# Placing every large SBUF buffer at a multiple of 64 bytes in a transformer block

## The reference

```python
mod = silu(c) @ ada_w.T + ada_b          # six vectors: shift, scale, gate for attention and for the MLP
h = rmsnorm(x) * g1 * (1 + scale_msa) + shift_msa
q, k, v = split(h @ qkv_w.T + qkv_b)     # q and k normalised per head, q scaled by 36 ** -0.5
o = softmax(q @ k.T) @ v
x = x + tanh(gate_msa) * (o @ proj_w.T + proj_b)
h2 = rmsnorm(x) * g2 * (1 + scale_mlp) + shift_mlp
x = x + tanh(gate_mlp) * (gelu(h2 @ fc1_w.T + fc1_b) @ fc2_w.T + fc2_b)
```

## Time and profile before

| | us |
|---|---|
| median of 3 runs | 3046.84 (3044.69 to 3047.96) |
| the profiled execution | 3046.41 |
| its span, first to last instruction | 3044.6 |
| TensorE matmul busy | 2963.3 (97%) |
| ScalarE busy | 1575.1 (52%) |
| VectorE busy | 1205.4 (40%) |
| GpSimd busy | 205.5 (7%) |
| mean granted clock of TensorE | 0.984 |

### The profile page before, as it was taken

The page is one execution under the profiler, slowest core; times in us unless marked ns, Lnnn a source line. Parts: engine busy times, 40 slices in busy tenths (PEclk is TensorE's granted clock), DMA queues, the critical chain, the costliest instruction groups (busy, mean ns, idle before and its releaser), DMA issues.

```text
span 3044.6 us, 36177 instructions
## 1 busy us (share of the span) xinstructions
PE 2963.3 (97%) x12968; PEld 1904.1 (63%) x12968; DVE 1205.4 (40%) x1540; ACT 1575.1 (52%) x1918; POOL 205.5 (7%) x126
## 2 busy tenths in 40 slices
PE   7999996999999999999999999999999999999998
PEld 7898993444444444444444444478888888888886
DVE  6878772333323323323323323434243342424332
ACT  3423323666666666666666666634343443434342
POOL 3232303520000000000000000000000000000000
PEclk7999997999999999999999999999999999999999
DMA  5454545232221222221222222121222222222121
GB/s 209 142 191 160 171 132 190 73 99 69 71 79 55 71 79 69 71 78 55 71 79 69 71 79 92 61 98 61 97 87 70 82 75 74 92 96 87 39 70 44
DMA packets 215540, 278.24 MB, mean 91 GB/s; under 512 B 15984, under 2 KB 125040, under 8 KB 214384
## 3 DMA queue, kind: packets, MB, share of 16 engines
q1 hardware_dynamic: 210160, 266.11, 27.4%
q10 hardware_dynamic: 5248, 10.49, 1.0%
HBM read 191.86 MB, written 84.67 MB: 91 GB/s over the span
## 4 chain that ended last, share of the span: by engine, by line
PE 80%; DVE 2%; DMA 1%; ACT 1%; SPq 0%; issue 0%; POOL 0%; DVEq 0%; POOLq 0%
PE ps L1255 23%; PE ps L1244 17%; PE ps L1305 15%; PE ps L1292 14%; PE ps L1254 7%; PE ps L1270 4%; ACT gated L1030 1%; DVE x L1162 0%; DMA vp<-v_scratch 0%; DVE rlb L1107 0%; DMA w_raw<-w 0%; DMA l_scratch<-osb 0%; DVE rlb L1101 0%; DVE w_lo L1156 0%; DVE x L1166 0%; DMA rlb<-l_scratch 0%
## 5 line engine op out<-in xcount | busy, mean ns | idle before, releaser
L983 ACT ACTIVATE prob<-ps 128x1024 f32<-128x1024 f32 x1084 | 979.4, 979 | 508.7 <-PE ps L1244 508.7
L1254 PE MATMUL ps<-prob,vp 128*64 128x512 f32 x2048 | 949.8, 601 | 1.4 <-DMA vp<-v_scratch 0.7
L1255 PE MATMUL ps<-prob,vp 128*37 128x512 f32 x2048 | 942.7, 598 | 0.0
L1244 PE MATMUL ps<-qT,kT 110*128 110x512 f32 x2048 | 564.4, 412 | 20.7 <-DMA qT<-m_scratch 19.4
L1244 PEld LDWEIGHTS ps<-qT,kT 110*128 110x128 f32 x2048 | 360.9, 189 | 346.4 <-ACT prob L983 193.5
L1255 PEld LDWEIGHTS ps<-prob,vp 128*37 128x37 f32 x2048 | 207.3, 114 | 389.2 <-issue 389.2
L1018 ACT ACTIVATE act<-ps,f1b_t 128x512 f32<-128x512 f32 x144 | 99.3, 689 | 518.8 <-PE ps L1292 518.8
L1095 DVE COPY osb<-ps 101x512 f32<-101x512 f32 x64 | 44.3, 692 | 753.4 <-PE ps L1255 750.2
L1254 PEld LDWEIGHTS ps<-prob,vp 128*64 128x64 f32 x2048 | 254.2, 136 | 118.4 <-issue 111.6
L1101 DVE RECIPROCAL rlb<-rlb 101x256 f32<-101x256 f32 x128 | 215.3, 1724 | 253.7 <-DMA rlb<-l_scratch 253.6
L1209 DVE TENSOR_TENSOR a_lo<-act,a_hi 128x512 fp32r<-128x512 f32 x144 | 99.6, 691 | 544.0 <-ACT a_hi L1020 544.0
(11 more groups left out here) (148 smaller groups left out, 2927.6 us busy)
## 6 DMA issues: line engine op xcount, KB each, us to landing
w_raw<-w SPq DMA_DIRECT2D x144, 320.0 KB, 2.8
qk_hi_scratch<-aw SPq DMA_DIRECT2D x32, 576.0 KB, 3.1
qk_lo_scratch<-aw SPq DMA_DIRECT2D x32, 576.0 KB, 4.4
kT<-qk_hi_scratch SPq DMA_DIRECT2D x128, 144.0 KB
qT<-qk_hi_scratch SPq DMA_DIRECT2D x128, 144.0 KB
v_scratch<-stv SPq DMA_DIRECT2D x32, 512.0 KB, 2.6
vp<-v_scratch SPq DMA_DIRECT2D x16, 1024.0 KB, 6.2
xb<-xT SPq DMA_DIRECT2D x8, 1280.0 KB, 10.0
```

Source lines behind the costliest of these rows:

```text
L983: act.activation(prob[:, slot, h0 * BLK:h1 * BLK], src, ACT.Exp).then_inc(exp_done, 1)
L1244: mm = pe.matmul(out, kT[r][:, h, kt * P:(kt + 1) * P], qT[:, c % 2, h], start=True, stop=True)
L1254: pe.matmul(O[0:64], vp[r][:, kt, 0:64], prob[:, j, 0:BLK], start=kt == 0, stop=kt == NT - 1)
L1255: pe.matmul(O[64:VW], vp[r][:, kt, 64:VW], prob[:, j, BLK:2 * BLK], start=kt == 0, stop=kt == NT - 1).then_inc(pv_mm, 1)
```

## The change

```diff
         def sb(stack, name, shape, dt=F32):
-            return stack.enter_context(nc.sbuf_tensor(name, shape, dt))
+            return stack.enter_context(nc.sbuf_tensor(name, shape, dt, align_bytes=64 if np.prod(shape[1:]) >= P else 32))
...
-    top = nc.sbuf_top
-    low_end = (nc.sbuf_base + 31) // 32 * 32
+    top = nc.sbuf_top // 64 * 64
+    low_end = (nc.sbuf_base + 63) // 64 * 64
...
     def following(name, shape, dt=F32):
         offset = here[0]
-        here[0] = offset + (4 * int(np.prod(shape[1:])) + 31) // 32 * 32
+        here[0] = offset + (4 * int(np.prod(shape[1:])) + 63) // 64 * 64
         return nc.alloc_sbuf_tensor_at(name, shape, dt, offset=offset)
...
     mo = following("mo", [P, 2 * NT])
+    SQ = here[0]
     mqx = following("mqx", [HD, P])
     mrow = following("mrow", [2 * NT, P])
+    here[0] = SQ
     sq0 = following("sq0", [P, 2, BLK], F32R)
```

## The result

| | before | changed |
|---|---|---|
| median of 10 runs, us | 3046.35 | 3037.99 |
| lowest to highest | 3043.76 to 3049.34 | 3034.03 to 3039.56 |
| the profiled execution, its span | 3046.41, 3044.6 | 3036.84, 3035.0 |
| ratio to before | | 0.9972, 95% interval 0.9963 to 0.9981 |

The change makes the kernel faster by 8.4 us (0.28%); 18 us had been forecast. The time lies in the wide range of 3020 to 3049 that was given, and outside the 3024 to 3034 of the forecast itself.

The account below looks back on a forecast made before the run. TensorE's matmul starts were taken to bound the MLP stage: fc2 13.4, fc1 3.8 and proj 0.8 us gave 18.0, all else 0, so 3046.84 - 18 = 3028.8 us. Range 3020 to 3049, the forecast's own 3024 to 3034.

Parts of the forecast that it names:

- the mismatch between weights and moving operand: MLP stage: fc2's weights start at 32, its moving operand at 0; this makes its step 233.3 ns, not 226.7.
- its bank order: fc2 changes its PSUM bank every three matmuls; the other possible cause of its slow step, which the prediction argued against.
- 13.4: MLP stage, fc2: 144 blocks falling from a mean of 3.267 to 3.174 us, 13.4 us saved.
- fc1's 3.8 us: MLP stage, fc1: 100 blocks of 3.21 and 36 of 3.18 us all falling to 3.174, 3.8 us saved.
- proj's 0.8: MLP stage, proj: 30 blocks falling from 3.20 to 3.174 us, 0.8 us saved.
- no new wait: MLP stage: about 1 us of cover is left between fc1 and fc2, so TensorE waits for nothing new.
- the 18.0 us: MLP stage: the savings of fc2, fc1 and proj together; every other stage was taken at 0 us.
- Rival 1: The change moves nothing TensorE feels: bank order or a coarser grid keeps fc2 slow; 3046.8 us within 2, chance 0.30.
- The argument from the qkv stage: For rival 1: half the qkv moving operands are 64 bytes off over 128, and 16.7 ns is the mean of 13.3 and 20.0.
- Rival 3: Mismatch gets worse: in a grid of 128 fc2 goes from 32 to 64 off, its price doubling; +13.5 us, 3060 us, chance 0.10.

Follow-up runs that it names:

- `qkv_only`: The kernel before with only the `sb` buffers at multiples of 64 and `main_phase` as before; ratio 0.9999.
- `w1_off_32`: The kernel before with 32 unused bytes before `w1_hi`, which also moves the buffers behind it, `a_hi` and `a_lo` among them; ratio 0.9998.
- `a_at_w2`: The kernel before with 224 unused bytes after `act32`, so only `a_hi` and `a_lo` move, nothing aligned at 64; 3038.52 against 3047.52 us, ratio 0.9970.
- the probe: The changed kernel plus runs of 24 matmuls behind the last fc2, at varied operand starts and widths (two such kernels); 226.7 ns a matmul at distance 0.
- `all_224`: The kernel before with attention and MLP buffers counted from below moved up 224 bytes, `sq0` overlapped as in the change; 3033.4 us, ratio 0.9952.
- `all_192`: The changed kernel with all buffers counted up from below moved up by 192 bytes; 3035.6 us, ratio 0.9956 to before.
- `all_128`: The changed kernel with the top at a multiple of 128 and the buffers from below moved up by 128 bytes; 3032.9 us, ratio 0.9951 to before.
- `top_128`: The changed kernel with the top of SBUF rounded to 128 bytes instead of 64; 3043.5 us, ratio 0.9985 to before.

## Why the prediction was right in sign and wrong in size

**What bounds the kernel, and that other edits cost nothing: right.** Attention, ScalarE, VectorE and the DMAs are unchanged, and `qkv_only` is at 1.00. The whole difference is fc2 and the blocks around it.

**That the mismatch between weights and moving operand makes fc2 slow, not its bank order: right, and now shown.** `w1_off_32` gives fc1 the slow step, `a_at_w2` takes it from fc2 with nothing more aligned, and two banks in turn cost nothing in the probe. The earlier trace rows had pointed to it.

**The step that failed: "With all operands of fc2 and proj at multiples of 64 I let every block of 14 run at 226.7 ns".** I took the difference in a grid of 64 bytes, so that a multiple of 64 on both sides would be a match. The grid is 256. After the change fc2's distance is 192, not 0, and its step went from 233.3 to 229.0 ns, 4.3 of the 6.7. Its blocks are 3.21 us, which is 144 x (3.267 - 3.213) = 7.8 us in place of 13.4. The hand-overs stay mismatched, so fc1's 3.8 us came out as 2.1 and proj's 0.8 as 0.3. That makes 10.2 us from the pieces, of which 0.8 went into longer waits at the starts of the blocks of columns, where the prediction had expected no new wait: 9.4 us, beside 9.5 in the trace of the stage and 8.4 in the medians. With a true match, `all_224`, `all_192` and `all_128`, the stage gives 16.3 to 16.9 of the 18.0 us: the arithmetic was nearly right for a layout that the change does not make. (It counts 36 of fc1's pieces of 3.18 us, where the chain has 38; that is under 0.1 us.)

**The sign was luck.** The match from which the gain was to come did not come about. The time fell because the change happened to put fc2 at 192, the one distance of the map beside a match that stays under 230 ns, with 229; at 16 to 96, 160 or 224 the probes have 233 to 234 ns, as before. `top_128`, at 128, gained half as much.

**The warning was in the text.** Rival 1 had said that over 128 bytes `w2_hi` and `a_hi` still differ; it was given no gain at all, and no rival priced a distance between the two levels. The argument from the qkv stage (16.7 ns as a mean of two levels) was no evidence either way: 432 columns follow another map. Rival 3, a price that grows with the distance to 64 or 128, is wrong in its form, since 16 to 96 cost the same within 1 ns; but `top_128` shows that a better aligned top can be the slower one.

**The Trainium skill's rule of two independent read ports by which TensorE would "never wait on anyone"** ("SBUF — State Buffer", "Who interferes with whom") gave the first rival its ground: the two reads can't disturb each other. The probe speaks against it. With every other engine and the DMAs idle, 24 matmuls take 5.45 us at distance 0 and 5.60 at 32, and only the start of the weights differs. The measurement decides. Whether the cost arises in the memory or inside TensorE was not measured.

## What to carry to other kernels

Where matmuls follow each other without a wait and each loads new weights, take the step from the starts and compare it between lines. Here a difference of 3% between lines of one shape came from where the operands stand. With 512 columns the starts of the weights and of the moving operand had to be multiples of 32 and to agree in their remainder by 256 bytes, over all operands that follow each other, and "a multiple of 64" was neither needed nor enough. 432 columns have another map, so measure it for the width at hand. A step measured at rest holds for a block of 14 only if the hand-overs keep that state.

## What the runs showed of the hardware beyond this

A float32r matmul of 512 columns with a weight load each came to rest at 226.7 ns at best at a granted clock of 1.00, 13.3 ns over its columns; 256, 384 and 448 columns at distance 0 took 120.0, 173.3 and 206.7 ns, which is 13.3 over the columns in the first two and 20.0 in the third. The slow steps are not random: they repeat in a fixed pattern (229, 232, 226 ns at distance 192, in the probe as in fc2 of the changed kernel), and after a mismatch the short step comes back only after some three to seven matmuls. Two starts both off a multiple of 32 cost 4 to 11 ns a matmul (231 ns at 8 bytes, 238 at 4), even with distance 0.
